# Written-out loops in five stages of a perceiver kernel on one Trainium2 core

## What is computed

```python
x = x + xattn(layernorm(x), ctx)                  # 16 heads, 257 context rows per batch
# second residual block (its halting steps collapse into one set of weights)
n = layernorm(x, g1, b1)
blended = ls1 * ((1 - alpha) * ssm(n) + alpha * gated_attention(n))
for e in range(8):                                # top 2 of 8, no capacity
    h = silu(flat @ W1[e]) * (flat @ W3[e])
    out = out + cw[:, e:e + 1] * (h @ W2[e])
x = x + weighted(x + blended + ls2 * out)
# third residual block: top 2 of 8, capacity 512 rows an expert
xg = xpad[buf]
h = gelu(einsum('ecd,edh->ech', xg, W1) + b1)
x = x + scattered(w * (einsum('ech,ehd->ecd', h, W2) + b2))
```

## Time and profile before

| | us |
|---|---|
| median of 3 runs | 1126.13 |
| lowest and highest run | 1125.68, 1127.5 |
| the profiled execution | 1125.93 |
| span of its trace | 1124.2 |
| mean granted clock of TensorE, share of full | 0.951 |

### The profile page before, as it was taken

How to read it: one execution, slowest core, us unless ns; L and a number is a source line. 1 busy time by engine, 2 the same in 40 slices (tenths; PEclk the granted TensorE clock), 3 DMA queues, 4 the chain that set the end, 5 groups by cost and what they waited for, 6 DMA issues and landing times. The chain is left out here.

```text
span 1124.2 us, 32342 instructions
## 1 busy us (share of the span) xinstructions
PE 1005.5 (89%) x10648; PEld 874.1 (78%) x10649; DVE 774.9 (69%) x2305; ACT 630.2 (56%) x1373; POOL 659.2 (59%) x813
## 2 busy tenths in 40 slices
PE   5899999999999997798999728999999627999998
PEld 3689889999899986687788516788887526988997
DVE  7577667767767776655566589676666486777884
ACT  2476676666666661633555477566665364444541
POOL 2477777777777781344666417767777203655443
PEclk9899999999999998899999859999999767999999
DMA  5221122221222212890000511333333348656501
GB/s 163 67 66 58 61 63 72 76 65 56 61 71 65 78 52 55 217 373 29 4 0 1 93 73 30 51 49 56 49 52 50 94 155 260 145 124 180 130 6 10
DMA packets 68555, 94.40 MB, mean 84 GB/s; under 512 B 12764, under 2 KB 48048, under 8 KB 68496
## 3 DMA queue, kind: packets, MB, share of 16 engines
q1 hardware_dynamic: 52464, 73.02, 20.4%
q0 software_dynamic: 16032, 20.62, 11.2%
HBM read 73.68 MB, written 22.18 MB: 85 GB/s over the span
## 5 line engine op out<-in xcount | busy, mean ns | idle before, releaser
L1926 POOL DMA_INDIRECT e_x<-rows,source x71 | 76.7, 1081 | 99.5 <-ACTq L1763 34.4
L652 ACT ACTIVATE xa_pr<-xa_pr,xa_nm 128x257 f32<-128x257 f32 x256 | 109.6, 500 | 21.3 <-DVE xa_nm L701 21.3
L635 ACT ACTIVATE xa_kT<-xa_kvp,xw_bk 128x258 fp32r<-128x258 f32 x128 | 60.8, 476 | 91.3 <-PE xa_kvp L465 83.9
L694 DVE TENSOR_SCALAR_CACHE_REDUCE xa_pr<-xa_sc 128x257 f32<-128x257 f32 x256 | 98.1, 422 | 13.2 <-PE xa_sc L490 7.7
L1937 POOL DMA_INDIRECT out_x<-e_y,target x32 | 54.2, 1694 | 73.7 <-DVE e_y L2724 61.6
L1931 POOL DMA_INDIRECT base<-e_y,place x39 | 72.8, 1867 | 36.4 <-DVE e_y L2214 23.7
L2561 PE MATMUL e_hb<-e_xTs,e_w1s 128*128 128x512 f32 x384 | 91.2, 398 | 1.9 <-issue 1.9
L2615 ACT ACTIVATE e_h<-e_hb,rc_F_b 128x512 f32<-128x512 f32 x64 | 44.0, 688 | 87.0 <-PE e_hb L2561 87.0
L597 POOL TENSOR_TENSOR xa_ol<-xa_om,xa_tl 128x256 f32<-128x256 f32 x64 | 46.7, 729 | 74.3 <-DVE xa_rinv L724 74.2
L2577 PE MATMUL e_yb<-e_w2s,e_hTs 128*128 128x256 f32 x768 | 89.1, 277 | 0.0
L705 DVE TENSOR_SCALAR xa_pT<-xa_ptp 128x512 f32<-128x512 f32 x128 | 87.5, 684 | 1.3 <-PE xa_ptp L500 1.1
(11 more groups left out here) (365 smaller groups left out, 2943.3 us busy)
## 6 DMA issues: line engine op xcount, KB each, us to landing
e_w<-in_F_W SPq DMA_DIRECT2D x16, 1024.0 KB, 8.7
w<-in_W SPq DMA_DIRECT2D x24, 512.0 KB, 9.6
xa_ctx<-in_ctxT SPq DMA_DIRECT2D x32, 257.0 KB, 3.1
xa_ctx<-in_ctxT SPq DMA_DIRECT2D x64, 128.5 KB, 3.1
xa_vb<-vlx SPq DMA_DIRECT2D x64, 128.0 KB
rows<-xs_oT SPq DMA_DIRECT2D x4, 516.0 KB, 9.7
xs_oT<-in_x SPq DMA_DIRECT2D x4, 512.0 KB, 5.7
base<-xs_oT SPq DMA_DIRECT2D x4, 512.0 KB, 3.2
```

The source lines that it names most:

```text
L652: act.activation(pr[:, par, g, :], pr[:, par, g, :], ACT.Exp, bias=nm[:, par, g:g + 1], scale=-1.0).then_inc(exp_ready, 1)
L694: dve.tensor_scalar(pr[:, par, g, :], sc[:, g, 0:S], CLAMP, None, ALU.min, ALU.min, accum_out=mx[:, par, g:g + 1]).then_inc(clip_ready, 1)
L1926: return pool.indirect_dma_start(out=out, out_offset=None, in_=rows, in_offset=bass.IndirectOffsetOnAxis(ap=index, axis=0))
```

## The change

In the five stages the three-part form (written-out head, hardware loop, written-out tail) becomes one plain loop at build time over all batches, steps, tiles or experts. Every semaphore count and address that came from the loop counter is a constant, and the jumps go. The expert numbers stay registers, and so does SP's context loop. One test on POOL in the cross-attention, which picked out the eight written-out batches by the type of the number, now names the same eight batches. The computation, its order on each engine and all waits stay.

```diff
--- before.py
+++ after.py
@@ -411,12 +411,7 @@
         block = st.enter_context(nc.Block(no_gpsimd_drain=True))
 
         def run_steps(eng, step, first, last):
-            for b in range(first, 4):
-                step(b, b % 2, b // 2)
-            with eng.Fori(1, B // 4 - 1) as i:
-                for j in range(4):
-                    step(i * 4 + j, j % 2, j // 2)
-            for b in range(B - 4, last):
+            for b in range(first, last):
                 step(b, b % 2, b // 2 % 2)
 
         def static(b):
@@ -612,7 +607,7 @@
                     last_value(b - 1, 1 - par, (2 * slot + par + 3) % 4)
                 if not static(b) or b < B - 2:
                     rest_of_context(pool, o, b + 2, par, 1 - slot)
-                if static(b):
+                if b < 4 or b >= B - 4:
                     c = b if b < 4 else b - B + 8
                     x = xs[:, T // 8 * c:T // 8 * c + T // 8, :]
                     pool.tensor_tensor(x, x, bo[:].unsqueeze(1).to_broadcast([P, T // 8, D]), ALU.add).then_inc(xs_ready, 1)
@@ -1087,11 +1082,8 @@
         beta_ready = p.sem("ss_beta_ready")
         block = st.enter_context(nc.Block(no_gpsimd_drain=True))
         def steps(eng, step):
-            for s in range(2):
-                step(s, s)
-            with eng.Fori(1, NS // 2) as i:
-                for j in range(2):
-                    step(i * 2 + j, j)
+            for s in range(NS):
+                step(s, s % 2)
 
         @block.sync
         def _(sp):
@@ -1272,12 +1264,7 @@
         block = st.enter_context(nc.Block(no_gpsimd_drain=True))
 
         def tiles(eng, step):
-            for t in range(-1, 3):
-                step(t, t % 2)
-            with eng.Fori(1, T // 2 - 2) as i:
-                for j in (1, 2):
-                    step(i * 2 + j, j % 2)
-            for t in range(T - 3, T + 2):
+            for t in range(-1, T + 2):
                 step(t, t % 2)
 
         def there(t, back):
@@ -2019,12 +2006,7 @@
         block = st.enter_context(nc.Block(no_gpsimd_drain=True))
 
         def tiles(eng, step, lag=0):
-            for j in range(E):
-                step(j, j % 2)
-            with eng.Fori(E // 2, J1 // 2 - 1) as i:
-                for j in range(2):
-                    step(i * 2 + j, j)
-            for j in range(2 * (J1 // 2 - 1), J1 + lag):
+            for j in range(J1 + lag):
                 step(j, j % 2)
 
         def static(j):
@@ -2488,12 +2470,7 @@
         block = st.enter_context(nc.Block(no_gpsimd_drain=True))
 
         def experts(eng, step):
-            for e in range(2):
-                step(e, e)
-            with eng.Fori(1, E // 2 - 1) as i:
-                for j in range(2):
-                    step(i * 2 + j, j)
-            for e in range(E - 2, E):
+            for e in range(E):
                 step(e, e % 2)
 
         def static(e):
```

## The result

The changed kernel takes 1118.94 us in the median of 4 runs (1118.65 to 1119.63), the kernel before 1126.82 us beside it (1125.68 to 1128.87): a ratio of 0.9926, 95% interval 0.9911 to 0.9941, some 8 us. The prediction had 1124.3 us. In two later series, on two chips, the same kernel came to 0.9918 [0.9901, 0.9935] and 0.9943 [0.9922, 0.9963].

The account below looks back on a forecast made before the run. PE was taken to bound the kernel, except in the first experts, where late gathers behind POOL's scatter-add did. Terms -2.8 + 0.6 - 2.6 + 3.2 = -1.6 us gave 1124.3 us, range 1118.8 to 1130.0.

Parts of the forecast that it names:

- Jumps in the cross-attention: Cross-attention on PE: 13 taken jumps, each on its path at 0.215 us, go; -2.8 us.
- Jumps elsewhere: State space, self-attention, second experts: PE's queued work hides the jumps; 0, at most 1.4 us further gain.
- Code in the self-attention: Self-attention on PE: written-out tiles need 9 more code fetches, some of which stall PE for 0.48 us; +0.6 us.
- the rate of one in seven: Self-attention: share of code fetches taken to stall PE, from one stall among 7 packets in a written-out stretch.
- The tie in the first experts: First experts: `e_w2s` on DVE and POOL's scatter-add start 0.01 us apart; DVE taken to come first; -2.6 us.
- the late pace: First experts: 5.26 us a tile in the loop once scatter-adds and gathers run late; 5.06 with the chain shortened.
- The rival with POOL first: First experts: scatter-add wins the tie, takes 1.62 us, PE bounds at 4.97 us a tile; 1119.8 us, chance 0.18.
- The price of a lost tie: First experts: a scatter-add behind `e_w2s` takes 2.54 us, ending 1.5 us after it; 5.06 us a tile.
- Code against gathers: First experts: some 7 code packets, 4 meeting a gather under way at half of 1.6 us; +3.2 us.
- One sign that the text set against itself: First experts: the prediction is wrong where gathers land late without code near them; no size given.
- The rule that crossing into new code is mostly hidden: Self-attention and first experts: by this skill rule both code terms, +0.6 and +3.2 us, would be nothing; the prediction set it aside.
- The rival in which code is dear and the whole is slower: Self-attention fetches all stall PE (+4.3), four gathers in the first experts are hit fully (+6.4); 1131.2 us, chance 0.17.

Follow-up runs that it names:

- e11: The changed kernel with only PE's first experts put back in the three-part loop; ratio to the kernel before 0.9954, 30 tiles in 152.42 us.
- e1: The kernel before with only the first experts written out, the other four stages still looped; 1125.29 us, ratio to the kernel before 0.9984.
- e16: The kernel before with only the first experts written out, a later repeat; ratio to the kernel before 0.9981.
- e13: The kernel before, loops kept, with three buffers for the first experts' gathered rows and PE's loop there in five passes of six tiles; 1121.89 us, ratio 0.996.
- e5: The changed kernel once more, unchanged, in a later series; ratio to the kernel before 0.9918.
- e10: The changed kernel with POOL's wait for the scaled output repeated four times ahead of each scatter-add; 1129.27 us, ratio to the kernel before 1.0013.
- e6: The changed kernel with 48 instructions that wait for nothing added ahead of PE's first experts; ratio to the kernel before 0.9977.
- e4: The kernel before with only state space, self-attention and second experts written out; ratio to the kernel before 1.0.
- e7: The changed kernel with six already satisfied waits ahead of each scatter-add on POOL, which delayed nothing; ratio to the kernel before 0.9934.
- e15: The kernel before with everything written out but the first experts, a repeat; ratio to the kernel before 0.9985.

## Why the prediction was wrong

- **Jumps in the cross-attention: right, a little small.** -2.8 was forecast, -3.43 measured, and the same 355.80 to 355.85 us in every kernel with that stage written out. A pass loses 0.26 us and not 0.215: the steps take 5.92 and 5.94 us in turn once written out, and the jump stands in one of the shorter ones, which the earlier trace rows set beside a longer one. The estimate of 1.4 us from the Trainium skill ("Advanced Engine Details and Errata", Control Flow Timing) is too low here by more than half.
- **Jumps elsewhere: right for the three stages, but the first experts have no such term.** State space and second experts are unchanged to 0.01 us a step. For the first experts the text put all of the 5.15 us a tile down to late gathers, and PE's 13 jumps there at nothing without saying so. From 727 to 826 us the loop's tiles take 4.97 and 5.13 us in turn, with no wait for a gather; this row of PE before follows the 774.20 and 779.17 of the earlier trace rows:

```profile
784.30 1.67 PE L2118 MATMUL e_yb<-e_w2s,e_hTs 128*128 128x256 f32 x12
```

  The change makes them 4.97 throughout, and e11 has its pairs of 5.10 and 4.97 back: 13 x 0.13 to 0.16, an estimated 1.7 to 2.1 us of the gain.
- **Code in the self-attention: wrong in sign, small.** +0.6 forecast, -0.54 measured: the one stall of the earlier trace rows is gone, and no new one came. But that isn't the change's. The step of 6.80 us that holds the stall is 6.53 us in e1 and e16 and 6.16, without a stall, in e13, which all keep this loop; and e5, the changed kernel again, has a stall of its own (PE), 88.38 us for the piece:

```profile
566.78 0.59 PE L1328 MATMUL sa_outb<-aw_Wout,sa_oT 128*128 128x256 f32 x2 [0.35 <-issue]
```

  So a stall of up to 0.5 us comes in some executions, looped or not, and the rate of one in seven was read from one case.
- **The tie in the first experts: this is the step that failed.** The text took it "that DVE comes first in every tile". The starts were forecast to a hundredth of a us, and the conclusion from them, that "the late pace becomes the pace of all tiles", was wrong: with both at the same time the scatter-add goes through in 1.62 us, and most tiles run at 4.97 us. In the kernel before, the late one of the earlier trace rows came 0.19 us behind `e_w2s`; a lead had shrunk to nothing, which is not the same as a lag. The 30 tiles were forecast at +0.6 us and gave -3.33: -0.98 in the first 21, where POOL led by 0.10 us before and PE's jumps go, and -2.35 in the last nine, in which the loop ran late. The rival with POOL first had 1119.8 us at a chance of 0.18, against 1118.94 measured. Its mechanism is the right one, but that its sum came so near is in part luck: it has nothing for the 1.83 us of the first 8 tiles and for the clock. What the Trainium skill says ("SBUF — State Buffer", Who interferes with whom), that issue order decides, agrees with e10; which of the two issues first in a tie, no row of before told, and the tie should have been weighed evenly.
- **The price of a lost tie: right for a tile, too small for the stage.** In the changed kernel's own late tiles `e_yb` starts at 829.74, 834.79 and 839.83 us, 5.05 apart, where 5.06 was forecast, and e10 has 5.07 without its waits for gathers. But those waits were 8.8 us there, against the +3.2 of the text: at a pace with no slack each late gather is paid in full, and seven tiles have one in every run. Had the tie gone to DVE in every tile, the forecast of 1124.3 would have been too fast.
- **Code against gathers: the mechanism is right, the ledger was one-sided.** +3.2 was charged for packets that meet gathers. In the changed kernel two waits of 1.3 us in all remain. What I left out is that the change also moves packets that the kernel before already met: the wait of 1.64 us in the earlier trace rows went, and with it most of the 1.83 us that the first 8 tiles gained. The tile of the earlier trace rows isn't a written-out one, as the text has it: PE turns tile 9 in the loop's first pass, whose code is as new as written-out code. One sign that the text set against itself did show: gathers land late without code near them, in the seven tiles named under e6.
- **The rule that crossing into new code is mostly hidden** (the Trainium skill, "Runtime: NRT & Kernel Launch", Instruction fetch mechanics) agrees with PE's own issue here: 89 packets, and no new stall in the cross-attention or the self-attention of this profile. The gathers that the packets meet pay all the same (e6).
- The rival in which code is dear and the whole is slower didn't come: e4, with the self-attention written out, is at 1.0, and the whole is faster.

## What to carry to other kernels

Writing a loop out is worth what its jump costs where an engine has nothing queued ahead (0.26 us a pass here), and nothing where it has. About as much was won in the 30 tiles of the first experts, from PE's jumps and from the register work in the chain that sets when a gather is issued. A third buffer, which lets each gather start a tile earlier, was worth as much in the looped stage, its passes on PE cut to five, as unrolling it (150.93 against 151.04 us for the 30 tiles), and brought the unrolled one to PE's pace, since it absorbs late landings from any cause. Before adding up parts of such a change, ask what each moves in the code of the stages behind it.

## What was not expected of the hardware

- Of two instructions that start together, POOL's scatter-add goes through as long as it starts at most 0.036 us behind the subtraction `e_w2s` on DVE (1.62 us, e7); from 0.050 us on (2.67 us, e15) it is held until 1.5 us after that ends. No run has a start between the two.
- A packet of code that starts 1.1 to 2.1 us after a gather's issue makes it land after 3.6 to 4.6 us in place of some 2.9; nearly all that start earlier or later leave it alone. So kernels that do the same work differ by where their code falls, by up to 1.7 us at a time; a reload of 2 MB may pay as well.
- The parts of the span outside the changed stages move by up to 4 us with the granted clock, which is 0.72 or 1.00 in the same operations; a difference of two single profiles is to be read stage by stage.
